# Routed rows of four neighbouring pages interleaved in memory, slot numbers turned to match

## The reference, cut to what matters

```python
logits = xf @ Wr + br                                  # 12288 tokens x 64 experts
topk_logits, topk_idx = jax.lax.top_k(logits, 2)
gates = jax.nn.softmax(topk_logits, axis=1)
combine = jnp.zeros((T, E), xf.dtype).at[jnp.arange(T)[:, None], topk_idx].add(gates)
for e in range(E):
    h = jax.nn.relu(xf @ W1[e] + b1[e])                # 64 -> 128
    y = h @ W2[e] + b2[e]                              # 128 -> 64
    out = out + combine[:, e:e + 1] * y
```

## Time and profile before

| what | before |
|---|---|
| median of three runs | 2414.56 us |
| the profiled execution, first to last instruction | 2525.0 us |
| POOL busy | 1087.2 us (43%) |
| DVE busy | 1618.5 us (64%) |
| PE busy | 1871.0 us (74%) |
| routing scatters, L1409 | 192, first start 1737.3, last 2021.7 us |
| expert stage, results L1953 | 64, first start 2044.3, last 2472.8 us |

### The profile page before, as it was taken

The page is one execution under the profiler, slowest core; times in us unless marked ns, Lnnn a source line. Parts: engine busy times, 40 slices in busy tenths (PEclk is TensorE's granted clock), DMA queues, the critical chain, the costliest instruction groups (busy, mean ns, idle before and its releaser), DMA issues.

```text
span 2525.0 us, 52330 instructions
## 1 busy us (share of the span) xinstructions
PE 1871.0 (74%) x16279; PEld 1453.1 (58%) x16279; DVE 1618.5 (64%) x5056; ACT 979.6 (39%) x3166; POOL 1087.2 (43%) x878
## 2 busy tenths in 40 slices
PE   5788887999999999999996477763333256666661
PEld 2257776777777777777774265552222155555561
DVE  0047773588888888888886799977888612222223
ACT  2277772344444444444442599862121100000000
POOL 0036660233434434344333322214888735555552
PEclk9989996899999999999995588885555555555555
DMA  9910000000000000000000000000000054434426
GB/s 276 292 51 0 0 0 1 2 2 2 1 0 0 0 0 0 0 0 0 0 1 1 0 1 1 1 1 11 23 22 23 24 159 111 115 111 113 114 74 158
DMA packets 119878, 106.65 MB, mean 42 GB/s; under 512 B 62448, under 2 KB 109680, under 8 KB 118896
## 3 DMA queue, kind: packets, MB, share of 16 engines
q1 hardware_dynamic: 87024, 73.88, 11.2%
q10 hardware_dynamic: 18432, 16.79, 2.2%
q0 software_dynamic: 14336, 14.91, 1.8%
HBM read 78.84 MB, written 26.67 MB: 42 GB/s over the span
## 4 chain that ended last, share of the span: by engine, by line
PE 30%; DVE 21%; issue 19%; POOL 11%; another core or an unknown queue 9%; ACT 2%; DMA 1%; DVEq 1%; ACTq 1%; SPq 0%; POOLq 0%
POOL routed_rows L1409 6%; PE PS L654 5%; PE PS L621 3%; PE PS L688 3%; PE PS L669 3%; PE PS L949 2%; POOL rstd L1310 2%; DVE XR L1563 2%; DVE XR L1763 1%; DVE XR L1559 1%; PE PS L941 1%; PE PS L703 1%; PE PS L728 1%; DMA arena<-expert_rows 1%
## 5 line engine op out<-in xcount | busy, mean ns | idle before, releaser
L1038 ACT ACTIVATE arena<-PS 128x384 f32<-128x384 f32 (+4 forms) x400 | 187.6, 486 | 665.4 <-remote 210.9
L1422 POOL DMA_INDIRECT expert_rows<-arena x256 | 245.2, 958 | 214.2 <-DVE arena L1953 141.7
L1943 DVE TENSOR_SCALAR arena<-PS 128x512 f32<-128x512 f32 x64 | 44.2, 691 | 359.8 <-remote 224.5
L1559 DVE TENSOR_REDUCE XR<-PS 128x2 f32<-128x192 f32 (+2 forms) x768 | 173.7, 280 | 105.0 <-PE PS L654 105.0
L654 PE MATMUL PS<-arena 32*128 32x96 f32 (+2 forms) x3072 | 234.1, 285 | 0.0
L1409 POOL DMA_INDIRECT routed_rows<-XR,SLu x192 | 199.7, 1040 | 75.0 <-issue 70.8
L949 PE MATMUL PS<-arena 128*128 128x64 f32 x512 | 126.0, 428 | 141.6 <-DVE arena L1943 140.7
L949 PEld LDWEIGHTS PS<-arena 128*128 128x128 f32 x512 | 114.0, 328 | 168.6 <-DVE arena L1943 142.6
L654 PEld LDWEIGHTS PS<-arena 32*128 32x128 f32 x3072 | 198.4, 192 | 20.7
L1355 POOL TENSOR_TENSOR arena<-arena,mhalf 96x16 f32<-96x16 f32 x32 | 93.3, 2915 | 241.6 <-DVE arena L1605 241.6
L1074 ACT ACTIVATE XR<-PS 128x256 f32<-128x256 f32 x512 | 167.3, 380 | 67.1 <-PE PS L669 66.9
(11 more groups left out here) (306 smaller groups left out, 4633.9 us busy)
## 6 DMA issues: line engine op xcount, KB each, us to landing
arena<-in_x_dram SPq DMA_DIRECT2D x32, 784.0 KB, 9.9
arena<-in_t_experts_dram ACTq DMA_DIRECT2D x128, 128.0 KB
arena<-in_t_experts_dram SPq DMA_DIRECT2D x128, 128.0 KB
routed_rows<-zt SPq DMA_DIRECT2D x16, 528.0 KB, 6.2
arena<-routed_rows SPq DMA_DIRECT2D x64, 132.0 KB
expert_rows<-arena POOLq DMA_INDIRECT x256
WP<-in_t_pack_dram SPq DMA_DIRECT2D x1, 3425.0 KB, 21.3
routed_rows<-XR,SLu POOLq DMA_INDIRECT x192
```

The source lines that it names most:

```text
L1038: return act.activation(dst, src, ACT.Identity, **kw)
L1422: pool.indirect_dma_start(YD, bass.IndirectOffsetOnAxis(yi[:, u % 4, k:k + 1], 0), yb[:, u % 4, k, :], None).then_inc(e_st[u % 2], 16)
L1559: dve.tensor_reduce(negmax[:, p, j, :], PS[:, S_:S_ + 2, S_AT[j]:S_AT[j] + QB * (j + 1)], AX_X, ALU.max, negate=True).then_inc(b_max, 1)
```

## The change

The rows of a group of four pages are laid out differently in `routed_rows`. Before, page k's row p stood at row 128 k + p of the group's 512. Now it stands at row 4 p + k. For partition p the four rows lie side by side, 4 x 264 = 1056 bytes, and the load of a group reads one run a partition where it read four. Where each row lands in `xb` is the same as before.

For this the slot number must be turned ahead of the scatter. With s the number as before, the new one is (s & ~511) | ((s << 2) & 508) | ((s >> 7) & 3). The cast from f32 goes to a new tile `SLi`; two ANDs, shifts and two ORs follow on DVE, three of the new steps linked, so `chain6` counts 17 links a turn. The expert stage's base of the same semaphore grows accordingly.

```diff
+        SLi = td("SLi", [P, 4, 2 * NV]).bitcast(U32)
@@ load_blocks
-                sp.dma_start(xb[:, u, :, :], XD[ds(g * (EB * SLOT), EB * SLOT)].rearrange("(k p) d -> p k d", p=P)
+                sp.dma_start(xb[:, u, :, :], XD[ds(g * (EB * SLOT), EB * SLOT)].rearrange("(p k) d -> p k d", p=P)
                              ).then_inc(e_in[u % 4], 16)
@@ d_places
-                link = Link(dve, chain6, g, 14)
+                link = Link(dve, chain6, g, 17)
...
                 dve.tensor_tensor(two, gde[:, u, 1, :], one, ALU.mult)
-                dve.tensor_copy(SLu[:, u, :, :].rearrange("p k b -> p (k b)"), TS_[:, :]).then_inc(d_slots, 1)
+                slot, row, page, group = (SLi[:, i, :] for i in range(4))
+                link(dve.tensor_copy(slot, TS_[:, :]))
+                dve.tensor_scalar(group, slot, 0xFFFF & -(EB * SLOT), None, ALU.bitwise_and)
+                dve.tensor_scalar(row, slot, 2, EB * SLOT - EB, ALU.logical_shift_left, ALU.bitwise_and)
+                link(dve.tensor_scalar(page, slot, 7, EB - 1, ALU.logical_shift_right, ALU.bitwise_and))
+                link(dve.tensor_tensor(row, row, page, ALU.bitwise_or))
+                dve.tensor_tensor(SLu[:, u, :, :].rearrange("p k b -> p (k b)"), group, row, ALU.bitwise_or).then_inc(d_slots, 1)
                 dve.tensor_tensor(tabx[:, :, :], tabx[:, :, :], tab1[:, :, :], ALU.add).then_inc(d_cell, 1)
@@ e_out
-                link.base += 2 * NR + 14 * NR
+                link.base += 2 * NR + 17 * NR
```

## The result

The changed kernel takes 2427.2 us (median of 20 runs), the one before 2415.1 us in the same comparison. The ratio is 1.0041, with a 95% interval from 1.0026 to 1.0056: slower by 6 to 14 us, 9.9 in the middle (the two medians lie 12.1 apart), forecast 10.1. Most of this study's numbers are profiles of single executions; ratios are of timed runs on one chip.

What follows compares the result with a forecast made beforehand. POOL was taken as the bound, in routing and through its stores in the expert stage. Slot numbers 0.79 us later over 16 turns, 12.6 us, less 2.5 of slack, added 10.1 to 2414.6: 2424.7 us, range 2413 to 2433.

Steps and rivals of the forecast that it cites:

- The sum: Routing: 12.6 us of later slot numbers less 2.5 us of slack, 10.1 us slower; load and scatter at 0.
- The chain of 0.79 us: Routing, DVE: six instructions replace one CAST, so slot numbers come 0.79 us later a turn, bounds 0.5 and 1.6.
- The slack: Routing: turns with more than POOL's 1.02 us from slot numbers to scatter absorb together 2.5 us of 12.6.
- The lower bound of 7.9: Routing: if signal to instruction took 0.88 us, 2.2 us less would be exposed, leaving 7.9 us.
- one of my signs: Routing: the gap from slot signal to scatter stays at 1.0 us; a turn lasts 18.6 to 18.8 us.
- Rival A: Routing: POOL prepares instructions behind running ones, hiding the delay but for the first turn; +1 to +3 us, 2417; 20%.
- Rival B: Routing: the POOL-DVE port holds a bitwise step every turn, 0.4 us more each; +16.5 us, 2431; 13%.
- What I had at nothing: Routing scatters: the same 192 scatters go to other addresses, taken as 0, one scatter's 1.26 us the bound.
- Rival C: Expert stage: loads set the timed pace, so 17 us come back and the kernel gains 7, 2407.5; 11%.
- The load at nothing: Expert stage: fewer, larger row packets save 4.2 us of DMA engine time a group, hidden by POOL's stores; taken as 0.
- The expert stage: POOL's stores set the timed pace, 5.05 us a group; most of 110.4 us are waits of the profiled execution.
- The room: Routing: DVE's 21.4 us of waiting for POOL's power only shift with the delay and take none of it back.

Runs made afterwards that it cites:

- e13: The changed kernel, unchanged, timed and profiled again on another chip beside the kernel before: ratio to before 1.0035.
- e12: The kernel before, unchanged, timed and profiled again: ratio to before 0.9981, median of the kernel before there 2415.1 us.
- e5: The changed kernel with its CAST, two ANDs, shift and OR done twice ahead of the slot signal: ratio to the kernel before 1.0094.
- e1: The changed kernel with the old row layout and six DVE instructions whose constants leave the slot number as it was: ratio to the kernel before 1.0047.
- e2: The kernel before with only the new load of one 1056-byte run a partition, slot numbers not turned: ratio to the kernel before 1.0006.
- group A: One of three groups of timed runs, each on one chip beside the kernel before, whose median in this group was 2515.1 us.
- e6: The kernel before with the five added DVE instructions behind the signal POOL waits for, results unused: ratio to the kernel before 1.0026.

## Why the prediction was right, and where it was wrong

**The sum.** Forecast 10.1 us in routing, measured 8.1 in the first pair of profiles, 8.6 by the medians of three, 10.1 in e13 against e12; timed 9.9 with an interval of 6 to 14. Sign, place and main mechanism hold: the slot numbers come later, POOL waits for them, and e5 pays in full for more. That the number fits as well as it does is partly luck. Two terms were off, and they nearly cancel: the slack was larger than the sum had it, and a share of the loss stood in it at nothing.

**The chain of 0.79 us** came out as 0.79 (median of 16 turns of the first profile, and of e1), up to 0.99 where L1928 was held.

**The slack.** I took 1.02 us from slot numbers to scatter as POOL's need, from the one turn where POOL was idle. In the changed kernel the step is 0.84 in nine turns and 0.92 to 0.94 in five; the other two are the first turn (1.02) and the third (1.14). It is the same in e1 and e13, turn by turn. So the turns had 4.5 us to give in the first pair and 5.9 on e12's chip, and not 2.5. That leaves 8.1 and 6.7 of the 12.6 us; POOL's first scatter of all and its gaps show 9.3 and 6.6. The lower bound of 7.9 was nearer to this part. e5 shows that beyond the slack all is paid. For the same reason one of my signs was wrong: the gap from slot signal to scatter did not stay at 1.0 us, and a turn lasts 18.54 us, just short of the 18.6 to 18.8 named.

**Rival A** (hidden by POOL) falls by e1 and e5: 1.0047 and 1.0094. **Rival B** (the port) asked for a bitwise step held in every turn. L1928 lasts 0.30 to 0.40 us in three turns of the first profile, 0.31 in one of e13 and never over 0.23 in e1, so this is small. The block lies where the first trace had it, in the later half of a scatter: L1928 ends at 1924.74 in a scatter of 1923.81 to 1924.77. What I had at nothing is the other direction: the scatters that wait for DVE's L1875 add 3.3 to 4.1 us to the loss in the three pairs of profiles. **Rival C** falls by e2.

**The load at nothing** holds: e2 at 1.0006. Its saving was over-estimated, 4.2 us of engine time a group for 2.7: 48 ns is what the weights' 1 KB packets took, and the 1056-byte ones took 64.

**The expert stage** was where I went wrong, without a cost to the sum. "I conclude that ... most of the 110.4 us between the span of 2525.0 and the median are these waits of the profiled execution" is false as to the cause: on the chip of group A the kernel before takes 2515 us in timed runs too, and a profiled execution takes at most 9.4 us more than the median of its kernel (e2), in e12 2408.1 for 2410.5. The profile's long waits did not shrink with the packets either (e2); the 2424.7 us of the profile after, which looked like it, is an execution without those waits. What held was the arithmetic behind it: 5.05 us a group forecast, 4.93 found for the results and 5.13 for the stores, which are the bound.

**The room.** "DVE's 21.4 us of waiting only shift" ignored that other stops live in that room (e6).

## What to carry to other kernels

An engine without a gap may be bound by its own work or by a loop that happens to close just in time; the step from the last input's signal to the instruction's start, compared with that step where the engine was idle, tells which. Take that step from several turns: the idle one had 1.02 us here, the busy ones 0.84 to 0.94. In the loop's case small steps ahead of the signal are paid in full once the slack is gone, and whether they are is settled cheaply by doing them twice. A shift of one engine against another can lengthen instructions that were not touched, so add up the durations as well as the gaps. A gain in DMA efficiency is worth what the DMA engines are waited for, here nothing. Before reading a span against a median, take a second profile of the same kernel.

## What the runs showed of the hardware that was not expected

- One and the same kernel took 2515 us in one group of timed runs and 2410 to 2415 in two others. The difference is almost all in the expert stage (428.5 against 311.5 us in its two profiles), as waits of some 7.8 us every second group.
- From a signal to the start of an indirect DMA on POOL passed 0.84 to 0.94 us in the middle turns, and 1.02 in the first turn after 19.46 us of idleness.
- An indirect DMA of POOL that starts while DVE's TENSOR_TENSOR on 128x768 is running (bf16 out, 0.96 us) ends 0.83 us behind it: 1.49 us long with 0.66 left, 1.58 with 0.75, 0.96 when alone.
- 264-byte packets took 21 ns and 1056-byte packets 64 ns of a DMA engine on average; merging four of the former saved 2.7 us of engine time a group, and nothing of the kernel's time that can be told (1.0006, 0.9986 to 1.0027).
